# Mixture-of-experts layer on one core: the tests for optional rows turned round

## The chip, the cores and the metric

One core of one Trainium2 chip runs the whole kernel in one launch. The core has a matmul engine (TensorE; PE in the profile, its weight loads PEld), a vector engine (DVE), a scalar engine (ACT), a general engine (POOL) and a sync engine (SP) that mostly issues DMAs. Each engine follows its own instruction list with a sequencer of its own; a trailing q (PEldq) marks a row of the sequencer. The metric is the device time of the launch in microseconds (us), as the median of several runs.

## The reference

An attention part and a mixture of experts over 4096 tokens of 512 numbers. Each token goes to 2 of 8 experts; an expert takes at most 1280 rows.

```python
x = x + _L0_xcond_ref(_layernorm(x), ctx_2048, ctx_2048, itok_B_779_1933)
x = x + _L0_ffn_ref(_layernorm(x), L0_ffn_Wg, L0_ffn_w1, L0_ffn_w2)

# _L0_ffn_ref, E = 8 experts, K = 2, C = 1280 rows at most
probs = jax.nn.softmax(xr @ Wg, axis=-1)
gate_vals, expert_idx = jax.lax.top_k(probs, K)
dispatched = xr[dispatch_mask.reshape(-1) % S].reshape(E, C, d)
h = jax.nn.relu(jnp.einsum('ecd,edf->ecf', dispatched, w1))   # 512 -> 2048
expert_out = jnp.einsum('ecf,efd->ecd', h, w2)                # 2048 -> 512
out = jnp.einsum('ks,ksm->sm', combine_weights, rerouted)
```

How many rows an expert really gets is known only while the kernel runs.

## The kernel before

The first part (to about 705 us of the span) is attention, routing and the writing of each token's row to a buffer ordered by expert. The second part, `experts`, is what the change touches. It handles the experts one after the other. An expert's rows come as two full tiles of T = 512 rows, numbered n = 2e and 2e + 1, and an optional rest of up to 256 rows, cut into ENDS = 4 end blocks of HP = 64 rows.

A full tile is done in NF = 16 steps. `up(n, f)` multiplies the rows with a piece of w1: 12 matmuls (four chunks, each as three products of high and low parts, lines 1408 to 1410), into the PSUM bank `ps_h`. ScalarE takes the relu (`relu`, line 1147, tile `hhi`), VectorE the low part (`low`, line 1269, tile `hlo`). `down(n, f)` multiplies these with a piece of w2: 12 matmuls (lines 1427 to 1429) into `ps_y`. On TensorE `up` of a step is written ahead of `down` of the step before, so that the other two engines work beside it.

After the first tile's steps (t = 0) the next tile's first `up(n + 1, 0)` is issued, and then comes the optional part. Here `rows`, a register that each of TensorE, VectorE and ScalarE loads for itself, is tested. The paths are:

- no rest (`rows <= 2 * T`): the tile's last `down(n, 15)`, then `end_skipped(e, 0)`, which counts three semaphores up (line 994) as the blocks would have;
- one block (up to 64 rows): `down(n, 15)`, `end_block(e, 0)` and `end_skipped(e, 1)`. On TensorE a block is 32 matmuls on w1 (line 1442), 16 transposes (line 1453) and 32 matmuls on w2 (line 1464). Its `end_skipped` waits until the counters show all of the block's work as done (`skipped`, the wait ahead of each increment), the last one `ed_done`, the end of line 1464's matmuls;
- four blocks: `down(n, 15)` and four times `end_block`.

Whichever path is taken, TensorE goes on with `up(n + 1, 1)` at its end. VectorE scales the finished tile (`y_out`, line 1311) and the end rows (`y_out_end`, lines 1319 to 1329); POOL adds them to the output with indirect DMAs.

The order on an engine is the order of the code: there is no scheduler. All three paths of an expert stand in the instruction list one behind the other, and branches choose among them. A branch to a path or to the code behind the paths is taken by the engine's sequencer; the engine itself works meanwhile on what the sequencer has already handed over. `down`'s first matmul in a block's `ps_y` waits on `y_ready` and `ey_ready` (the wait of line 1425 and the one above it).

Of the kernel before, what the change touches and what calls it, by code (L numbers as in the profile page):

```python
# [24 lines left out]
T = 512  # L25
TB = T // P
NF = FF // P
# [13 lines left out]
HP = P // 2  # L41
# [843 lines left out]
def experts(nc, w1, w2, out_rows, disp, totals, fill, spare, raw, raw_ld, xin, xin_ld):  # L885
    N = 2 * E
    with ExitStack() as stack:
# [238 lines left out]
        @block.scalar  # L1126
        def _(act):
            def cut(e, i):
                k = PIECES * e + i
                act.wait_ge(raw_ld[k % NRAW], 16 * (k // NRAW + 1))  # L1130
                nc.scalar.activation(piece(w1hi, w2hi, i), raw_view(raw, k), ACT.Copy).then_inc(w_hi, 1)

            def x_high(n, c):
                if n == 0:
                    act.wait_ge(x0_done, c + 1)
                else:
                    act.wait_ge(xt_done, NC4 * (n - 1) + c + 1)
                nc.scalar.activation(xhi[n % 2][:, c, :], (ps_y[c] if n == 0 else ps_x)[:], ACT.Copy).then_inc(xhi_ready, 1)

            def end_high(e, half):  # L1140
                act.wait_ge(ex_done[half], e + 1)
                nc.scalar.activation(ex[:, :, :, 0, :], ex_rows, ACT.Copy).then_inc(ehi_ready[half], 1)

            def relu(n, f):
                k = NF * n + f
                act.wait_ge(h_done, k + 1)
                nc.scalar.activation(hhi[k % 2][:], ps_h[k % 3][:], ACT.Relu).then_inc(hhi_ready, 1)  # L1147

            def end_moved(e, j, q):
                m = NC4 * (ENDS * e + j) + q  # L1150
                act.wait_ge(eu_done, m + 1)
                if j or q >= 2:
                    act.wait_ge(et_done, m - 1)
                nc.scalar.activation(hrow[q % 2], end_bank(2 * e, q)[HP:P, :], ACT.Copy).then_inc(eu_moved, 1)

            def end_cols(e, j, q):
                m = NC4 * (ENDS * e + j) + q
                act.wait_ge(et_done, m + 1)
                if j or q >= 2:
                    act.wait_ge(ed_done, m - 1)  # L1160
                nc.scalar.activation(eh[q % 2][:, :, 0, :], eh_rows, ACT.Relu).then_inc(ehh_ready, 1)

            def end_block(e, j):
                if j == 2:
                    end_high(e, 1)
                end_moved(e, j, 0)
                end_moved(e, j, 1)
                end_cols(e, j, 0)
                end_moved(e, j, 2)
                end_cols(e, j, 1)  # L1170
                end_moved(e, j, 3)
                end_cols(e, j, 2)
                end_cols(e, j, 3)

            def end_skipped(e, j):
                if j <= 2:
                    skipped(act, ehi_ready[1], e, 1)
                skipped(act, eu_moved, NC4 * (ENDS * e + j), NC4 * (ENDS - j))
                skipped(act, ehh_ready, NC4 * (ENDS * e + j), NC4 * (ENDS - j))

            for i in range(2):
                cut(0, i)
            for c in range(NC4):
                x_high(0, c)
            for e in range(E):
                rows = rows_of(act, e)
                for t in range(2):
                    n = 2 * e + t
                    for f in range(NF):
                        if not (t == 1 and f == 0):  # L1190
                            relu(n, f)
                        if n == 0 and f % 2 == 0 and f < NF - 2:
                            cut(0, f + 2)
                            cut(0, f + 3)
                        if f in XAT and n + 1 < N:
                            x_high(n + 1, XAT.index(f))
                        if t == 0 and f == ENDAT:
                            end_high(e, 0)
                        if t == 0 and e >= 1 and f == 1:
                            cut(e, PIECES - 2)  # L1200
                            cut(e, PIECES - 1)
                        if t == 1 and e + 1 < E and f % 2 and f >= 3:
                            cut(e + 1, f - 3)
                            cut(e + 1, f - 2)
                    if t == 0:
                        relu(n + 1, 0)
                        with act.If(rows > 2 * T):
                            with act.If(rows > 2 * T + HP):
                                for j in range(ENDS):
                                    end_block(e, j)  # L1210
                            with act.Else():
                                end_block(e, 0)
                                end_skipped(e, 1)
                        with act.Else():
                            end_skipped(e, 0)

        @block.vector
        def _(dve):
# [118 lines left out]
            for e in range(E):  # L1337
                rows = rows_of(dve, e)
                for t in range(2):
                    n = 2 * e + t  # L1340
                    for f in range(NF):
                        if not (t == 1 and f == 0):
                            low(n, f)
                        if t == 0 and f == 0 and e >= 1:
                            y_out(n - 1)
                        if n == 0 and f % 2 == 0 and f < NF - 2:
                            cut(0, f + 2)
                            cut(0, f + 3)
                        if f + 1 in XAT and n + 1 < N:
                            x_turn(n + 1, XAT.index(f + 1))  # L1350
                        if f in XAT and n + 1 < N:
                            x_low(n + 1, XAT.index(f))
                        if t == 0 and f == ENDAT - 1:
                            end_turn(e, 0)
                        if f == 3 and n + 1 < N:
                            keep_gates(n + 1)
                        if t == 0 and f == ENDAT:
                            end_low(e, 0)
                            keep_end_gates(e)
                        if t == 0 and e >= 1 and f == 1:  # L1360
                            cut(e, PIECES - 2)
                            cut(e, PIECES - 1)
                        if t == 1 and e + 1 < E and f % 2 and f >= 3:
                            cut(e + 1, f - 3)
                            cut(e + 1, f - 2)
                    if t == 0:
                        low(n + 1, 0)
                        with dve.If(rows > 2 * T):
                            y_out(n)
                            with dve.If(rows > 2 * T + HP):  # L1370
                                for j in range(ENDS):
                                    end_block(e, j)
                                    y_out_end(e, j)
                            with dve.Else():
                                end_block(e, 0)
                                y_out_end(e, 0)
                                end_skipped(e, 1)
                        with dve.Else():
                            end_skipped(e, 0)
                            y_out(n)  # L1380
            y_out(N - 1)

        @block.tensor
        def _(pe):
# [98 lines left out]
            def end_skipped(e, j):  # L1483
                skipped(pe, eu_done, NC4 * (ENDS * e + j), NC4 * (ENDS - j))
                skipped(pe, et_done, NC4 * (ENDS * e + j), NC4 * (ENDS - j))
                skipped(pe, ed_done, NC4 * (ENDS * e + j), NC4 * (ENDS - j))
# [3 lines left out]
            for e in range(E):  # L1490
                rows = rows_of(pe, e)
                for t in range(2):
                    n = 2 * e + t
# [6 lines left out]
                            down(n - 1, NF - 1)  # L1500
                    if t == 0:
                        up(n + 1, 0)
                        with pe.If(rows > 2 * T):
                            with pe.If(rows > 2 * T + HP):
                                down(n, NF - 1)
                                for j in range(ENDS):
                                    end_block(e, j)
                            with pe.Else():
                                down(n, NF - 1)
                                end_block(e, 0)  # L1510
                                end_skipped(e, 1)
                        with pe.Else():
                            down(n, NF - 1)
                            end_skipped(e, 0)
            for b in range(TB):
                down(N - 1, NF - 2, [b])
                down(N - 1, NF - 1, [b])
# [21 lines left out]
```

## Time and profile before

| what | value |
|---|---|
| median of 3 runs | 2215.71 us (2215.48 to 2218.86) |
| the profiled execution's own time | 2217.91 us |
| its span, first to last instruction | 2216.2 us |
| TensorE busy (matmuls) | 2128.2 us, 96% |
| VectorE, ScalarE, POOL busy | 45%, 33%, 21% |
| mean granted TensorE clock | 0.988 of full |

The span is what the trace covers; 1.7 us of the execution's own time lie around it. TensorE's share is that of matmul records, which overlap a little. The share of the whole hides that the two parts differ: in the first, engines wait for each other, in the second TensorE stands almost without a pause.

### The profile page before, as it was taken

What the parts mean: (1) busy time and instruction counts of PE and PEld (TensorE: products, weight loads), DVE (VectorE), ACT (ScalarE), POOL (GpSimd) and SP (SyncE); (2) the same over time, 40 slices, a digit from 0 to 9 for tenths busy, and PEclk for the clock granted to TensorE, in tenths of its full rate; (3) what the DMA queues carried; (4) which work ended last, traced back from release to release, by engine and by line L of the source; (5) the groups of instructions that cost most, each with busy time, mean ns of one, the idle gap of its engine ahead of it and who ended that gap; (6) DMA issues with size and microseconds to landing.
All of it is one profiled execution on the core that took longest, in us unless ns stands there. A gap on an engine that the chain in (4) does not pass through costs nothing. (4 is left out here: it accounts for less than half of the span.)

```text
span 2216.2 us, 27023 instructions
## 1 busy us (share of the span) xinstructions
PE 2128.2 (96%) x10226; PEld 1524.4 (69%) x10226; DVE 1000.8 (45%) x1872; ACT 727.2 (33%) x1246; POOL 471.2 (21%) x595
## 2 busy tenths in 40 slices
PE   3899999999995999999999999999999999999997
PEld 1445555455544888877888888888888788888776
DVE  5577787777754434323423423432432342343211
ACT  1566666666662323212212211321321221132110
POOL 3133434434323110310201021031030102101101
PEclk9999999999996999999999999999999999999999
DMA  8987877788833444321612523432251252341101
GB/s 132 148 164 161 176 168 155 178 165 180 156 110 128 127 97 124 70 40 59 149 25 58 125 49 58 123 67 38 90 122 21 59 125 48 58 124 29 16 6 19
DMA packets 180724, 218.60 MB, mean 99 GB/s; under 512 B 35472, under 2 KB 107160, under 8 KB 180537
## 3 DMA queue, kind: packets, MB, share of 16 engines
q1 hardware_dynamic: 150852, 174.85, 36.6%
q0 software_dynamic: 22240, 37.92, 8.9%
q10 hardware_dynamic: 7476, 3.75, 1.0%
q8 instruction: 99, 1.62, 0.3%
q14 instruction: 57, 0.46, 0.1%
HBM read 113.93 MB, written 68.29 MB: 82 GB/s over the span
## 5 line engine op out<-in xcount | busy, mean ns | idle before, releaser
L1269 DVE SCALAR_TENSOR_TENSOR hlo<-ps_h,hhi 128x512 fp32r<-128x512 f32 x256 | 177.1, 692 | 931.2 <-ACT hhi L1147 879.1
L1147 ACT ACTIVATE hhi<-ps_h 128x512 fp32r<-128x512 f32 x256 | 152.9, 597 | 1123.5 <-PE ps_h L1410 1084.4
L1427 PE MATMUL ps_y<-w2hi,hhi 128*128 128x512 f32 x1024 | 404.8, 395 | 3.2 <-issue 2.5
L1408 PE MATMUL ps_h<-xhi,w1hi 128*128 128x512 f32 x1024 | 404.5, 395 | 1.3 <-PEq L994 1.3
L1429 PE MATMUL ps_y<-w2hi,hlo 128*128 128x512 f32 x1024 | 404.3, 395 | 0.0
L1428 PE MATMUL ps_y<-w2lo,hhi 128*128 128x512 f32 x1024 | 403.8, 394 | 0.0
L581 DVE TENSOR_REDUCE nmax<-ps_s 128x1 f32<-128x512 f32 x512 | 338.0, 683 | 145.3 <-PE ps_s L784 137.5
L1410 PE MATMUL ps_h<-xhi,w1lo 128*128 128x512 f32 x1024 | 403.6, 394 | 0.0
L1409 PE MATMUL ps_h<-xlo,w1hi 128*128 128x512 f32 x1024 | 403.3, 394 | 0.0
L435 ACT ACTIVATE probs<-ps_t 128x512 f32<-128x512 f32 x512 | 280.3, 600 | 197.2 <-PE ps_t L794 138.1
L1428 PEld LDWEIGHTS ps_y<-w2lo,hhi 128*128 128x128 f32 x1024 | 193.1, 189 | 48.5 <-issue 2.7
L1408 PEld LDWEIGHTS ps_h<-xhi,w1hi 128*128 128x128 f32 x1024 | 192.3, 188 | 47.9 <-issue 2.6
L784 PE MATMUL ps_s<-kst,qst 96*128 96x512 f32 x416 | 190.7, 469 | 35.7 <-DMA qst<-qlo 29.6
L1427 PEld LDWEIGHTS ps_y<-w2hi,hhi 128*128 128x128 f32 x1024 | 192.7, 188 | 46.6 <-DVE hlo L1269 1.1
L1429 PEld LDWEIGHTS ps_y<-w2hi,hlo 128*128 128x128 f32 x1024 | 192.6, 188 | 46.1
L1409 PEld LDWEIGHTS ps_h<-xlo,w1hi 128*128 128x128 f32 x1024 | 192.7, 188 | 45.5
L1410 PEld LDWEIGHTS ps_h<-xhi,w1lo 128*128 128x128 f32 x1024 | 192.3, 188 | 46.0
L1082 POOL DMA_INDIRECT out_x<-y,ids x64 | 103.4, 1616 | 455.4 <-DVE y L1311 441.0
L784 PEld LDWEIGHTS ps_s<-kst,qst 96*128 96x128 f32 x416 | 82.0, 198 | 145.6 <-DVE nmax L581 67.3
L794 PE MATMUL ps_t<-qst,kst 104*128 104x512 f32 x416 | 169.2, 412 | 3.7 <-ACT probs L435 1.6
L1064 POOL TENSOR_TENSOR ids<-xtail,zeros 128x4 int32<-128x4 int32 x15 | 5.5, 365 | 713.3 <-DMA xtail<-dispatched 713.3
L767 PE MATMUL ps_o<-probs,vt 128*32 128x512 f32 x1024 | 137.2, 608 | 0.0
(160 smaller groups left out, 2018.0 us busy)
## 6 DMA issues: line engine op xcount, KB each, us to landing
raw<-in_L_ffn_w SPq DMA_DIRECT2D x128, 512.0 KB
qst<-qhi SPq DMA_DIRECT2D x64, 256.0 KB
xin<-dispatched SPq DMA_DIRECT2D x60, 256.0 KB, 5.9
kst<-khi SPq DMA_DIRECT2D x52, 256.0 KB
xt<-in_x SPq DMA_DIRECT2D x32, 256.0 KB, 3.7
ct<-in_ctx SPq DMA_DIRECT2D x32, 256.0 KB, 3.3
qst<-qlo SPq DMA_DIRECT2D x32, 256.0 KB
xres<-in_x SPq DMA_DIRECT2D x32, 256.0 KB, 3.5
```

Of the source, the lines that this page charges most:

```text
L435: nc.scalar.activation(probs[n % 3][:, i, :], ps_t[(k - 1) % 3][:], ACT.Exp).then_inc(t_free, 1)
L581: nc.vector.tensor_reduce(nmax[s % 2][:, i, c:c + 1], ps_s[(k - 1) % 3][:], AX, ALU.max, negate=True).then_inc(s_free, 1)
L784: nc.tensor.matmul(bank[:], qst[s % KR][0:STACK, c, cols], kst[s % KR][0:STACK, c, :], start=True, stop=True).then_inc(s_done, 1)
L794: nc.tensor.matmul(bank[:], kst[g % KR][0:STACK + MROWS, i, cols], qst[g % KR][0:STACK + MROWS, i, :], start=True, stop=True).then_inc(t_d ...
L1147: nc.scalar.activation(hhi[k % 2][:], ps_h[k % 3][:], ACT.Relu).then_inc(hhi_ready, 1)
L1269: nc.vector.scalar_tensor_tensor(hlo[k % 2][:], ps_h[k % 3][:], 0.0, hhi[k % 2][:].bitcast(F32), ALU.max, ALU.subtract).then_inc(h_ready, 1)
L1408: nc.tensor.matmul(to, w1hi[:, c, fs], xhi[n % 2][:, c, :], start=(c == 0), stop=False)
L1409: nc.tensor.matmul(to, w1hi[:, c, fs], xlo[n % 2][:, c, :], start=False, stop=False)
L1410: done = nc.tensor.matmul(to, w1lo[:, c, fs], xhi[n % 2][:, c, :], start=False, stop=(c == NC4 - 1))
L1427: nc.tensor.matmul(ps_y[b][:], hhi[k % 2][:, bs], w2hi[:, f, :], start=(f == 0), stop=False)
L1428: nc.tensor.matmul(ps_y[b][:], hhi[k % 2][:, bs], w2lo[:, f, :], start=False, stop=False)
L1429: done = nc.tensor.matmul(ps_y[b][:], hlo[k % 2][:, bs], w2hi[:, f, :], start=False, stop=(f == NF - 1))
```

## The change

The tests are written the other way round on ScalarE, VectorE and TensorE, and their bodies change places. Each path contains the same operations in the same order; which rows take which path is unchanged. What changes is where each path stands in the instruction list and which path is reached or left by a jump.

```diff
@@ block.scalar
                         relu(n + 1, 0)
-                        with act.If(rows > 2 * T):
-                            with act.If(rows > 2 * T + HP):
+                        with act.If(rows <= 2 * T):
+                            end_skipped(e, 0)
+                        with act.Else():
+                            with act.If(rows <= 2 * T + HP):
+                                end_block(e, 0)
+                                end_skipped(e, 1)
+                            with act.Else():
                                 for j in range(ENDS):
                                     end_block(e, j)
-                            with act.Else():
-                                end_block(e, 0)
-                                end_skipped(e, 1)
-                        with act.Else():
-                            end_skipped(e, 0)
@@ block.vector
                         low(n + 1, 0)
-                        with dve.If(rows > 2 * T):
+                        with dve.If(rows <= 2 * T):
+                            end_skipped(e, 0)
                             y_out(n)
-                            with dve.If(rows > 2 * T + HP):
+                        with dve.Else():
+                            y_out(n)
+                            with dve.If(rows <= 2 * T + HP):
+                                end_block(e, 0)
+                                y_out_end(e, 0)
+                                end_skipped(e, 1)
+                            with dve.Else():
                                 for j in range(ENDS):
                                     end_block(e, j)
                                     y_out_end(e, j)
-                            with dve.Else():
-                                end_block(e, 0)
-                                y_out_end(e, 0)
-                                end_skipped(e, 1)
-                        with dve.Else():
-                            end_skipped(e, 0)
-                            y_out(n)
@@ block.tensor
                         up(n + 1, 0)
-                        with pe.If(rows > 2 * T):
-                            with pe.If(rows > 2 * T + HP):
+                        with pe.If(rows <= 2 * T):
+                            down(n, NF - 1)
+                            end_skipped(e, 0)
+                        with pe.Else():
+                            with pe.If(rows <= 2 * T + HP):
+                                down(n, NF - 1)
+                                end_block(e, 0)
+                                end_skipped(e, 1)
+                            with pe.Else():
                                 down(n, NF - 1)
                                 for j in range(ENDS):
                                     end_block(e, j)
-                            with pe.Else():
-                                down(n, NF - 1)
-                                end_block(e, 0)
-                                end_skipped(e, 1)
-                        with pe.Else():
-                            down(n, NF - 1)
-                            end_skipped(e, 0)
```

Per expert TensorE's list holds the four-block path (332 matmuls), the one-block path (92) and the path without a rest (12). A matmul is two instructions there, a weight load and the multiplication. With the waits and increments between them the four-block path is 686 instructions long, the one-block path about 190, the shortest about 28.

First place: TensorE, at the first expert's tests, behind `up(1, 0)`. Before:

```order
L1410 MATMUL ps_h<-xhi,w1lo 128x512
L1503 COMPARE_AND_BRANCH
L1504 COMPARE_AND_BRANCH
L1427 MATMUL ps_y<-w2hi,hhi 128x512
L1428 MATMUL ps_y<-w2lo,hhi 128x512
```

Now:

```order
L1410 MATMUL ps_h<-xhi,w1lo 128x512
L1503 COMPARE_AND_BRANCH
L1427 MATMUL ps_y<-w2hi,hhi 128x512
L1428 MATMUL ps_y<-w2lo,hhi 128x512
L1429 MATMUL ps_y<-w2hi,hlo 128x512
```

Before, the matmuls that follow the tests belong to the four-block path; now they belong to the path without a rest, and the second test stands behind that path.

Second place: TensorE, where the one-block path ends (line 1464 is its last product). Before:

```order
L1464 MATMUL ps_y<-w2hi,xhi 128x512
L1464 MATMUL ps_y<-w2lo,xhi 128x512
L1508 UNCONDITIONAL_BRANCH
L1427 MATMUL ps_y<-w2hi,hhi 128x512
L1428 MATMUL ps_y<-w2lo,hhi 128x512
```

Now:

```order
L1464 MATMUL ps_y<-w2hi,xhi 128x512
L1464 MATMUL ps_y<-w2lo,xhi 128x512
L1507 UNCONDITIONAL_BRANCH
L1427 MATMUL ps_y<-w2hi,hhi 128x512
L1428 MATMUL ps_y<-w2lo,hhi 128x512
```

The rows read alike, but what the branch passes over differs. Before, behind it stands the path without a rest (12 matmuls); now the four-block path (332 matmuls).

Third place: TensorE, where the path without a rest ends. Before:

```order
L1427 MATMUL ps_y<-w2hi,hhi 128x512
L1428 MATMUL ps_y<-w2lo,hhi 128x512
L1429 MATMUL ps_y<-w2hi,hlo 128x512
L1512 UNCONDITIONAL_BRANCH
L1408 MATMUL ps_h<-xhi,w1hi 128x512
```

Now:

```order
L1427 MATMUL ps_y<-w2hi,hhi 128x512
L1428 MATMUL ps_y<-w2lo,hhi 128x512
L1429 MATMUL ps_y<-w2hi,hlo 128x512
L1503 UNCONDITIONAL_BRANCH
L1507 COMPARE_AND_BRANCH
```

Before, this path stood last and its branch led to the next instruction, `up(n + 1, 1)` (line 1408). Now it stands first and its branch leads past both other paths.

## Rows read from the trace of the kernel before

**Rows 1.** The page, part 1: busy us (share of the span), instructions

```profile
PE 2128.2 (96%) x10226; PEld 1524.4 (69%) x10226; DVE 1000.8 (45%) x1872; ACT 727.2 (33%) x1246; POOL 471.2 (21%) x595
```

**Rows 2.** Waits of the matmul engine from 716 us to the end

```profile
PE ps_y L1427 <- issue: 2.5, 1, 2.5
PE ps_h L1408 <- PEq L994: 1.3, 3, 0.4
PE ps_y L1427 <- DVE hlo L1269: 0.7, 1, 0.7
```

**Rows 3.** Windows: length, then busy us (count) of each engine, PEclk

```profile
core 0: us, PE busy (x) PEld busy (x) DVE busy (x) ACT busy (x) POOL busy (x), PEclk, DMA share, GB/s
1184.00:1355.00 171.00, 171.00 (x736) 137.67 (x735) 58.26 (x74) 38.08 (x56) 27.19 (x23) 1.00 0.37 81
800.99:805.15 4.16, 4.16 (x20) 3.37 (x18) 0.11 (x1) 0.00 (x0) 0.00 (x0) 1.00 0.03 8
1354.96:1359.13 4.17, 4.17 (x19) 3.35 (x18) 0.10 (x1) 0.00 (x0) 0.00 (x0) 1.00 0.02 4
2093.94:2098.27 4.33, 4.33 (x13) 3.37 (x13) 2.07 (x3) 0.00 (x0) 1.45 (x1) 0.61 0.01 4
```

**Rows 4.** Groups by line: one end block's first product

```profile
L1442 PE MATMUL ps_h<-w1hi,ex 128*128 128x512 f32 x48 | 19.6, 408 | 0.0
```

**Rows 5.** Source L1503, TensorE's sequencer: ns min/median/max, first and last start

```profile
L1503 PEldq COMPARE_BRANCH  x8: 82/3316/3632, 801.0 to 2087.2; - x8
```

**Rows 6.** Source L1504, the second test's branch

```profile
L1504 PEldq COMPARE_BRANCH  x3: 3338/3373/3573, 979.3 to 2087.3; - x3
```

**Rows 7.** Source L1508, the branch at an end block's end

```profile
L1508 PEldq COMPARE_BRANCH  x3: 185/185/190, 1003.6 to 2115.8; - x3
```

**Rows 8.** Source L1503 from 800 to 802 us

```profile
L1503 PEldq COMPARE_BRANCH  x1: 3307/3307/3307, 801.0 to 801.0; - x1
```

**Rows 9.** DMA from 800.99 to 804.30 us, during that branch

```profile
q8 instruction: 1, 0.02, 1.7%
```

**Rows 10.** DMA from 1003 to 1005 us, around an L1508 branch

```profile
DMA packets 0, 0.00 MB, mean 0 GB/s; under 512 B 0, under 2 KB 0, under 8 KB 0
```

**Rows 11.** Source L1207: ScalarE's first branch

```profile
L1207 ACTq COMPARE_BRANCH  x8: 40/45/53, 805.4 to 2091.5; - x8
```

**Rows 12.** Timeline around 2091 us: start, length, instruction [idle before]

```profile
2091.09 0.40 PE L1410 MATMUL ps_h<-xhi,w1lo 128*128 128x512 f32 x1
2091.09 0.19 PEld L1427 LDWEIGHTS ps_y<-w2hi,hhi 128*128 128x128 f32 x1
...
2093.94 0.39 PE L1427 MATMUL ps_y<-w2hi,hhi 128*128 128x512 f32 x1 [2.46 <-issue]
```

**Rows 13.** DMA from 2090.68 to 2094.20 us

```profile
q8 instruction: 1, 0.02, 2.4%
```

**Rows 14.** DMA from 1184 to 1355 us, 736 matmuls and 735 loads

```profile
q8 instruction: 6, 0.10, 0.2%
```

**Rows 15.** Timeline around 1003 us, the end of an end block

```profile
1003.04 0.40 PE L1464 MATMUL ps_y<-w2lo,xhi 128*128 128x512 f32 x1
...
1003.88 0.50 PE L1408 MATMUL ps_h<-xhi,w1hi 128*128 128x512 f32 x1 [0.44 <-PEq L994]
...
1004.99 0.48 DVE L1329 TENSOR_SCALAR y_end<-y_part,end_gates 64x512 f32<-64x512 f32 x1
```

**Rows 16.** Source L994 from 1179.3 to 1180 us

```profile
L994 PEldq EVENT_SEMAPHORE  x3: 51/51/51, 1179.4 to 1179.7; - x3
```

**Rows 17.** Timeline at 97 us, TensorE

```profile
97.07 0.50 PE L784 MATMUL ps_s<-kst,qst 96*128 96x512 f32 x1 [4.41 <-DVE nmax L581]
```

**Rows 18.** Windows: 97.5 to 104.3 us, PEclk the third from the right

```profile
97.50:104.30 6.80, 6.64 (x24) 2.27 (x22) 2.98 (x5) 2.39 (x5) 1.64 (x3) 0.50 0.99 153
```

## The prediction

> **What bounds the kernel now.** I read the page's first part: TensorE is busy 96% of the span, no other engine half of it [rows 1]. That is an average over two parts, so I went to TensorE's waits from 716 us on, the part that the change touches [rows 2]. The reader is to see three rows with 4.5 us in all: one wait of 2.5 us ended by "issue" (no engine was late, the instruction itself was), three of 0.4 us behind an end block, and one of 0.7 us at the end. So a microsecond that TensorE loses there is a microsecond of the result, and nothing else in it matters unless it makes TensorE wait. A window inside the part gives the step: 736 matmuls in 171.0 us, 0.232 us each, at the full granted clock [rows 3].
>
> Next: which path do the experts take? Line 1442's first product ran 48 times [rows 4] and a block has 16 of them: three blocks. The first test ran eight times [rows 5], the second three times [rows 6]. So three experts (tests at 979, 1713 and 2087 us) have one block, five have none, and none has four.
>
> Then the branches of TensorE's sequencer. Three of the first tests (the minimum of 82 ns) were not taken; the five that jumped over the blocks took up to 3632 ns [rows 5], and the three second tests, which jump over the four-block path, took 3338, 3373 and 3573 ns [rows 6]. The branch behind a block, which passes only the path without a rest, took 185 to 190 ns [rows 7]. The first long one (3307 ns, [rows 8]) has one packet of an instruction queue, 0.02 MB, inside it [rows 9]; around a short one there is no DMA at all [rows 10]. I read this as: a jump far ahead leaves the instructions that the sequencer holds and waits until a block of them has been read from memory, 3.3 to 3.6 us. The branch of line 1512 has no record: it led to the next instruction. ScalarE's branches took 40 to 53 ns [rows 11]; its paths are short, VectorE's too, and they were jumped over before as well, so I put both engines at nothing. If one of them had a far jump, its 3.3 us would show in TensorE's wait for `ey_ready`.
>
> The Trainium skill ("Runtime: NRT & Kernel Launch", Instruction fetch mechanics) says that a taken branch to a target outside the current two pages forces a DMA of the target page before execution goes on. The trace agrees (3307 ns and one packet against 185 ns and none). The same section gives TensorE room for 2048 instructions, by which a jump over 686 could land in what is there; that reading is rival B.
>
> **What hid these 3.3 us.** The sequencer runs ahead of the engine. When the first long branch began, TensorE had 4.16 us of work before it, and when the fourth expert's began 4.17 us (18 matmuls at 0.232; [rows 3]). 3.31 to 3.63 us fit below that, and TensorE did not stop. It stopped once, in the last expert's second test: the branch ended at 2087.30 + 3.37 = 2090.67, one weight load passed at 2091.09, and the matmul that belongs to it started at 2093.94 [rows 12], with a second instruction packet in between [rows 13]. A packet holds some 250 instructions (six packets in a stretch of 736 matmuls and 735 loads, [rows 14]); the jump's target lay one or two instructions ahead of the end of such a packet, so the sequencer had to wait for the next one, until 2093.94 − 2090.67 = 3.27 us after the branch.
>
> **The change, part by part.**
>
> (a) The stall of the last expert goes. Its second test now falls through, and the first jumps only over the 28 instructions of the short path, as the 0.19 us branches did. Gained: 2093.94 − 2091.09 = 2.85, less one step of 0.23: 2.62 us. Behind the stall the granted clock was at its lower level (1.2 instead of 2.4 GHz, mean 0.61 over the window): 12 steps took 4.33 us instead of 12 × 0.232 = 2.79 [rows 3]. That is 1.54 us more. Sum −4.16.
>
> (b) The three one-block experts now leave the block by a jump over 686 instructions. Nothing covers it: `end_skipped` waits for `ed_done`, that is until line 1464's last matmul has finished, so the queue is empty when the branch comes. In the first block: last matmul started at 1003.04, next matmul 1003.88 [rows 15], the branch of 0.19 us right ahead of it. The price is a long branch instead of a short one. I take the three of line 1504, which jump over the same code: 3.34 + 3.37 + 3.57 − 3 × 0.19 = +9.7 us. Bounds: 3 × (3.31 − 0.19) = 9.4 and 3 × (3.63 − 0.19) = 10.3. Behind the branch wait `up(n + 1, 1)`, and with it ScalarE and VectorE; no engine has other work for TensorE. VectorE's end rows, done at 1004.99 + 0.48 = 1005.47 [rows 15], are ready before TensorE resumes at about 1007.1, so their wait costs nothing.
>
> (c) The clock after (b). TensorE now idles 0.6 + 3.2 = 3.8 us at each of three places. After 2.6 us of idleness it fell once, for 1.54 us of loss; after 4.4 us at 97 us [rows 17] it stayed at the lower level for 6.8 us [rows 18], which at this step would cost twice as much, 3.1; after the 0.6 us pauses it did not fall. So the price of each place lies between 0 and 3.1. I take the nearest row, 1.54, in two of three places, since that fall does not tell me where the limit is: +3.1 in all.
>
> (d) The five experts without a rest. Before, the far branch stood ahead of `down(n, 15)`; now behind it and behind three increments, which come 0.15 us apart, 0.35 us together [rows 16]. `down` replaces `up` as cover: 4.16 − 0.35 = 3.8 us against branches of 3.31 to 3.63. Price 0, at most 0.1 each if the longest branch meets the shortest cover. If the cover were gone, each would cost what (b) does, 3.2.
>
> (e) A second packet after a jump. All eight far jumps now land at `up(n + 1, 1)`. Placing the packets' ends by the stall at 2091 us and counting instructions, I get at least 39 instructions to the end of the packet at every landing, the least in the last expert. 39 instructions are 19 matmuls or 4.5 us, more than the 3.27 us that the second packet takes. Price 0; if the count is off, up to 4.2 us at one landing.
>
> Sum: −4.2 + 9.7 + 3.1 + 0 + 0 = +8.6 us. Against the profiled execution's own 2217.9 us that is 2226.5. That execution lies 2.2 us above the median of the runs shown, so I put the sum on the median: 2215.7 + 8.6 = 2224.3 us. The lower end of the costs (no clock fall, 9.4) gives +5.2, so 2220.9; the upper end with every place at 1.54 and 10.3 gives +10.7, so 2226.4, and 2229 if the stall of (a) is not in the unprofiled runs. That mechanism's own range is thus 2220.5 to 2229.5.
>
> **Rivals.**
>
> A. Exposed further: the far branch of the five short paths is not covered after all, or a landing is short of instructions. For: the margin of (d) is 0.2 us where a branch takes 3.6. Against: the cover was the same 4.16 to 4.17 us in two experts and the sequencer's lead does not depend on which matmuls fill it. Price: one landing 4.2, or pauses of 0.1 to 1 us with a lower clock after some; 2224.3 + 5 = about 2229. Chance 0.12.
>
> B. Not slower: the jump behind the block is as cheap as it was. This would be so if TensorE's sequencer kept the code that it has passed over, or if a branch without a test had its target read ahead. It is decided at one place, the branch behind line 1464: if it takes 0.19 us, (b) and (c) vanish and (a) stays, 2215.7 − 4.2 = 2211.5, just within 0.2%. Against it: all eight jumps over 686 instructions or more took 3.3 us and more. For it: no unconditional branch of this length is in the trace. Chance 0.08.
>
> C. Half of it: the branch overlaps with the drain (its target is asked for while `ed_done` is still awaited), or the clock never falls and the branches are at their shortest, so that less than 4.4 us is left. 2215.7 + 3 = 2218.7. Nothing in the trace speaks for the overlap; the short branch began after the last increment. Chance 0.08.
>
> **How the numbers follow.** The forecast holds 0.72, A 0.12, B 0.08, C 0.08. 0.2% (4.4 us) is about what a measurement of this kernel can tell from no change. Forecast and A are slower by more, 0.84, with a third of C 0.86; faster by more needs B and a little luck, 0.02; the rest, 0.12, is within. The range that leaves out 2 in 10 is 2219 to 2230: it takes in both ends of (b) and (c), and A.
>
> **What will show it.** The changed profile should have three records of line 1507's unconditional branch of 3.3 to 3.6 us, each with an instruction packet inside, and TensorE's wait ahead of line 1408 at 3.6 us three times instead of 0.4. The five of line 1503's short path should be as long without any pause of TensorE. The wait of 2.5 us at line 1427 should be gone and the first test's record in one-block experts about 0.19 us. PEclk should be below 1 for some 3.4 us behind two or three of the pauses. It would be wrong if line 1507's branch took 0.2 us, or if pauses appeared behind line 1503.

## The result and the profile after

The changed kernel takes 2229.09 us (median of 6 runs, 2224.41 to 2231.65) against 2216.18 us before (6 runs, 2215.07 to 2218.92). The ratio is 1.0052, 95% interval 1.0037 to 1.0067: slower by 8 to 15 us. The forecast was 2224.3 us in a range of 2219 to 2230, with 0.86 on slower. The profiled execution took 2231.13 us, its span 2229.4 us, 13.2 us over the span before.

TensorE's waits of the changed kernel from 716 us on:

```profile
PE ps_h L1408 <- issue: 11.2, 3, 3.9
PE ps_y L1427 <- DVE hlo L1269: 0.7, 1, 0.7
```

Of [rows 2] the single wait of 2.5 us at line 1427 is gone, and the three of 0.4 us at line 1408 have become three of 3.5 to 3.9. These are the branches of line 1507 behind the three end blocks; the sequencer's rows, each from a stretch of its own (ns, then first and last start):

```profile
L1507 PEldq COMPARE_BRANCH  x1: 3265/3265/3265, 1003.1 to 1003.1; - x1
L1507 PEldq COMPARE_BRANCH  x1: 3516/3516/3516, 1741.9 to 1741.9; - x1
L1507 PEldq COMPARE_BRANCH  x1: 3643/3643/3643, 2122.6 to 2122.6; - x1
```

[Rows 7] had 185 to 190 ns for the branch at that place. Inside the first of them, 1003.1 to 1006.3 us, one instruction packet was read, and a second in the 2.6 us behind it (the two DMA views):

```profile
q8 instruction: 1, 0.02, 1.9%
```

```profile
q8 instruction: 1, 0.02, 3.0%
```

The timeline around the first, beside [rows 15]:

```profile
1002.50 0.40 PE L1464 MATMUL ps_y<-w2lo,xhi 128*128 128x512 f32 x1
1003.00 0.69 DVE L1319 COPY y_part<-ps_y 64x512 f32<-64x512 f32 x1 [3.15 <-PEq L994]
...
1004.44 0.48 DVE L1329 TENSOR_SCALAR y_end<-y_part,end_gates 64x512 f32<-64x512 f32 x1
...
1006.41 0.79 PE L1408 MATMUL ps_h<-xhi,w1hi 128*128 128x512 f32 x1 [3.51 <-issue]
1007.00 0.63 PE L1409 MATMUL ps_h<-xlo,w1hi 128*128 128x512 f32 x1
...
1007.43 0.63 PE L1410 MATMUL ps_h<-xhi,w1lo 128*128 128x512 f32 x1
```

VectorE is through at 1004.92; nothing but the sequencer holds TensorE back until 1006.41. Then the matmuls come 0.43 us apart instead of 0.23. The windows behind the three pauses, up to the first step at full speed (length, busy us and count by engine, PEclk third from the right):

```profile
1006.41:1012.44 6.03, 6.03 (x15) 4.74 (x15) 0.00 (x0) 0.51 (x1) 2.33 (x2) 0.51 0.13 17
1745.46:1749.69 4.23, 4.23 (x12) 3.31 (x13) 0.00 (x0) 0.00 (x0) 1.53 (x1) 0.60 0.16 22
2126.34:2131.98 5.64, 5.64 (x14) 4.44 (x14) 0.00 (x0) 0.11 (x1) 1.73 (x2) 0.51 0.16 22
```

The granted clock was at its lower level (1.2 instead of 2.4 GHz) behind all three. The five experts without a rest show no pause. The first one's far branch took 3397 ns and ended at 802.85 + 3.40 = 806.25, and `up(n + 1, 1)` followed `down(n, 15)` at the usual step:

```profile
L1503 PEldq COMPARE_BRANCH  x1: 3397/3397/3397, 802.8 to 802.8; - x1
```

```profile
806.29 0.39 PE L1429 MATMUL ps_y<-w2hi,hlo 128*128 128x512 f32 x1
806.52 0.40 PE L1408 MATMUL ps_h<-xhi,w1hi 128*128 128x512 f32 x1
```

In the three experts with a block line 1503's branch now passes only the short path; in the first of them it took 263 ns, and the stall of [rows 12] is nowhere:

```profile
L1503 PEldq COMPARE_BRANCH  x1: 263/263/263, 978.5 to 978.5; - x1
```

### The profile page after: what moved, and what is told of

The parts are those of the page before. It is cut to its first block and busy times, and to the rows that moved or that the text cites. A ratio compares the mean times of both kernels' runs of the same rounds, so it can differ in the third digit from the quotient of the medians.

```text
span 2229.4 us, 27038 instructions
## 1 busy us (share of the span) xinstructions
PE 2134.1 (96%) x10226; PEld 1526.3 (68%) x10226; DVE 998.6 (45%) x1872; ACT 727.2 (33%) x1246; POOL 471.7 (21%) x595
```

## The experiments

Each ratio is to the kernel before, measured on the same chip beside the variant: median 2216.93 us for the first four, 2219.11 us for the others. The spread between single runs of one kernel is up to 14 us, so where one place is in question its rows are read, not the times.

**Which engine: TensorE alone.**

```diff
 # block.tensor as in the changed kernel; block.scalar and block.vector as before
-                        with pe.If(rows > 2 * T):
+                        with pe.If(rows <= 2 * T):
```

> Only TensorE's tests are turned round, ScalarE's and VectorE's stay as before. My theory (the loss is TensorE's uncovered far jump behind an end block, and the granted clock after it): as in the changed kernel, +9 to +14 us over before, three pauses of 3.9 to 4.3 us ahead of line 1408. Rival (the other engines' new jumps delay what TensorE waits for): under +4 us.

Measured: 2227.65 us, ratio 1.0053 (1.0040 to 1.0067), the same as with all three engines (1.0052). Waits of TensorE:

```profile
PE ps_h L1408 <- issue: 12.0, 3, 4.1
PE ps_y L1427 <- DVE hlo L1269: 0.7, 1, 0.7
```

**The other two engines alone.**

```diff
 # block.scalar and block.vector as in the changed kernel; block.tensor as before
-                        with act.If(rows > 2 * T):
+                        with act.If(rows <= 2 * T):
```

> Only ScalarE's and VectorE's tests are turned round, TensorE's stay as before. My theory: no difference from before, within 1.5 us, and TensorE's stall of 2.6 us in the last expert is still there. Rival (those engines carry part of the loss): +3 us or more.

Measured: 2216.37 us, ratio 1.0005 (0.9996 to 1.0015), no difference. The stall of the last expert is there:

```profile
PE ps_y L1427 <- issue: 3.0, 1, 3.0
PE ps_h L1408 <- PEq L994: 1.3, 3, 0.4
```

Together the two say that the loss is in TensorE's list; what the other two engines add is at most the 3 us that the second interval leaves (1.0015).

**Distance: the code that is jumped over made short.** In this kernel TensorE's four-block path does one block; no expert takes it here.

```diff
                             with pe.Else():
                                 down(n, NF - 1)
-                                for j in range(ENDS):
-                                    end_block(e, j)
+                                end_block(e, 0)
+                                end_skipped(e, 1)
```

> The changed kernel, with TensorE's four-block path (that no expert takes here) cut to one block, so 192 instructions instead of 686; for an expert that needs four blocks it would leave three out. The jump behind an end block passes 192 instructions instead of 686. My theory (price by distance: outside what the sequencer holds): the three branches of line 1507 fall from 3.3 to 3.6 us to 0.2, the clock falls there vanish, and with the last expert's old stall gone too the time is 3 to 5 us under before. Rival 1 (an unconditional or second branch costs 3.3 us whatever it passes): still +9 us or more. Rival 2 (the pause is the drain of ed_done that the profile puts on the branch): pauses as long as in the changed kernel.

Measured: 2213.81 us, ratio 0.9988 (0.9976 to 1.0001), 14 us under the changed kernel by the two ratios (1.0052 − 0.9988, of 2216). Against before that is −2.7 us (−5.3 to +0.2), a little less than the 3 to 5 expected and hardly told from no change. The profiled run has no pause as in the changed kernel, and no fall of the clock: its steps of over 0.3 us lose 3.4 us less than those of the kernel before. The branches behind the blocks took 308 to 313 ns, not the 0.2 us expected, and TensorE's waits there are up to 0.7 us; this is the first branch, and the waits:

```profile
L1507 PEldq COMPARE_BRANCH  x1: 312/312/312, 999.6 to 999.6; - x1
```

```profile
PE ps_h L1408 <- PEq L994: 1.8, 3, 0.7
```

So the 3.3 us are not in a branch without a test, nor in the drain, but in how far ahead the branch leads. The same run has a finer answer in the five experts without a rest, where the jump now leads 385 instructions ahead, more than one packet and less than two:

```profile
L1503 PEldq COMPARE_BRANCH  x1: 3489/3489/3489, 799.4 to 799.4; - x1
```

```profile
L1503 PEldq COMPARE_BRANCH  x1: 3793/3793/3793, 1174.6 to 1174.6; - x1
```

```profile
L1503 PEldq COMPARE_BRANCH  x1: 309/309/309, 1353.8 to 1353.8; - x1
```

```profile
L1503 PEldq COMPARE_BRANCH  x1: 765/765/765, 1532.7 to 1532.7; - x1
```

```profile
L1503 PEldq COMPARE_BRANCH  x1: 308/308/308, 1908.8 to 1908.8; - x1
```

One and the same jump took 0.3, 0.8 or 3.5 to 3.8 us. I count instructions in the built list from the packet's end that the stall at 2091 us gives, with 256 to a packet (the number is worked out below, at the kernel with 24 increments). By that count the two dear ones land in the next packet but one and the three others in the next. The one of 765 ns started nine instructions behind a packet's end; that the next packet was still on its way is my reading and was not tested. What counts is how many packets a jump goes ahead, not its length. The same count sorts every jump of TensorE behind 716 us in all ten profiles: within its packet 185 to 267 ns, into the next 292 to 313 ns (and the 765), further 3265 to 3892 ns. It also says why the branches behind the blocks took 0.3 us here and 0.19 before: they now cross one packet's end.

**Alignment: everything 32 instructions later.**

```diff
                     for f in range(NF):
+                        if n == 0 and f == 8:
+                            for _ in range(PAD):        # PAD = 32
+                                pe.sem_inc(pad, 1)
                         if not (t == 1 and f == 0):
                             up(n, f)
```

> The kernel before with 32 semaphore increments more on TensorE's list in the first expert, so that everything behind them lies 32 instructions later. My theory (the stall at the last expert's jump comes from a target one or two instructions ahead of the end of a fetched packet): the target now lies some 226 instructions ahead of an end, the 2.6 us stall and the 3.4 us of lower clock vanish, 3 to 5 us under before; the 32 increments take 1.6 us of the sequencer and are hidden by its lead of 4.1 us. Rival (the stall is a wait for another engine or a slow read of instructions in that place): it stays, no difference or +1 us.

Measured: 2211.20 us, ratio 0.9979 (0.9968 to 0.9989), 4.7 us (2.4 to 7.1) under before. The 32 increments were not quite hidden; TensorE waited 0.7 us for them:

```profile
PE ps_h L1410 <- PEq L996: 1.3, 3, 0.4
PE ps_y L1429 <- DVE hlo L1271: 0.7, 1, 0.7
PE ps_h L1410 <- issue: 0.7, 1, 0.7
```

(Lines are two further down in this kernel.) The stall at line 1427, now 1429, is gone.

**Alignment: 24 instructions, to bring the stall back elsewhere.**

```diff
-PAD = 32
+PAD = 24
```

> As the kernel with 32 increments, but 24. By my count of instructions the last expert's target then lies 234 instructions ahead of a packet's end, and the target in the sixth expert (at about 1717 us) two. My theory: no stall at 2091, and one of 2.6 to 3.2 us ahead of line 1427's first matmul behind the sixth expert's test instead. Rival (32 increments helped for another reason): no stall anywhere, or still at 2091.

There is one execution of it (2222.49 us), the profiled one; a single time says nothing here, the place is what counts. The sixth expert's test, timeline of TensorE:

```profile
1718.78 0.39 PE L1412 MATMUL ps_h<-xhi,w1lo 128*128 128x512 f32 x1
1721.96 0.39 PE L1429 MATMUL ps_y<-w2hi,hhi 128*128 128x512 f32 x1 [2.79 <-issue]
```

It is the only long wait of that run's second part. The stall moved from the eighth expert to the sixth, as counted. It also gives the packet's length. An expert takes 2444 instructions of the list before, so from the one place to the other it is 2 × 2444 − 24 = 4864 instructions. Both targets lie just ahead of a packet's end, so this is a whole number of packets, and near the 250 of [rows 14] only 19 × 256 fits.

**Cover: work beside the far jump of the changed kernel.**

```diff
-                        if not (t == 1 and f == 0):
+                        if not (t == 1 and f < 2):
                             up(n, f)
...
                                 end_block(e, 0)
+                                up(n + 1, 1)
                                 end_skipped(e, 1)
```

and the same line ahead of `end_skipped(e, 0)` and behind the four blocks.

> The changed kernel with up(n + 1, 1), 12 matmuls or 2.8 us, moved from behind the paths to the end of each path, ahead of end_skipped, so that TensorE has work while the far jump is taken. My theory: the pauses behind the three end blocks shrink by about 2.8 us, from 3.3 to 3.7 of idleness beyond the old 0.6 to about 1 us each, with fewer falls of the clock; in the sixth expert the jump by my count lands 7 instructions ahead of a packet's end, so there a second wait of about 2.5 us comes on top. Time 3 to 9 us under the changed kernel. Rival (the time goes to the branch whatever runs beside it): as the changed kernel.

Measured: 2219.74 us, ratio 1.0002 (0.9993 to 1.0011). By the two ratios that is 0.5%, 11 us (7 to 15), under the changed kernel, at the upper end of the 3 to 9 expected or above it. In the profiled pair the steps of over 0.3 us lose 9.9 us less. Waits:

```profile
PE ps_y L1427 <- issue: 2.9, 3, 1.2
PE ps_y L1429 <- issue: 2.6, 1, 2.6
```

The branches are as long as ever (3297, 3672 and 3292 ns), but three waits of up to 1.2 us are left of 3.5 to 3.9. The second row is the short landing in the sixth expert; only there did the clock fall:

```profile
1736.99 0.47 PE L1427 MATMUL ps_y<-w2hi,hhi 128*128 128x512 f32 x1 [1.23 <-issue]
1737.30 0.39 PE L1428 MATMUL ps_y<-w2lo,hhi 128*128 128x512 f32 x1
1740.28 0.59 PE L1429 MATMUL ps_y<-w2hi,hlo 128*128 128x512 f32 x1 [2.59 <-issue]
```

**The same cover in the kernel before.** The edit is the same, in the old order of the paths.

```diff
                                 end_block(e, 0)
+                                up(n + 1, 1)
                                 end_skipped(e, 1)
```

> The kernel before with up(n + 1, 1) moved likewise into the paths. It covers the drain behind an end block: the three pauses of 0.6 us go (1.8 us in all). The move makes each expert's part of TensorE's list longer; by my count the stall of 2.6 us or more then stands in the second expert (at about 980 us) and no longer in the last. Time 1 to 3 us under before. Rival: the stall stays at 2091 us.

Measured: 2216.65 us, ratio 0.9989 (0.9979 to 0.9999), 2.4 us (0.2 to 4.7) under before. The pauses behind the blocks are gone and the stall stands in the second expert:

```profile
978.93 0.40 PE L1410 MATMUL ps_h<-xhi,w1lo 128*128 128x512 f32 x1
981.50 0.39 PE L1427 MATMUL ps_y<-w2hi,hhi 128*128 128x512 f32 x1 [2.17 <-DVE hlo L1269]
```

The profile names VectorE's `hlo` here, as the last semaphore of this wait:

```profile
980.00 0.69 DVE L1269 SCALAR_TENSOR_TENSOR hlo<-ps_h,hhi 128x512 fp32r<-128x512 f32 x1 [4.88 <-ACT hhi L1147]
```

That `hlo` belongs to `up(n + 1, 0)`, which this matmul does not read, and it was done at 980.69, 0.8 us before the matmul started. By this and by the count the wait is the sequencer's here too. A smaller wait, 0.6 us, is left in the sixth expert, whose jump lands 18 instructions ahead of a packet's end. It was not forecast.

**Cover and alignment together.** The calls of `up(n + 1, 1)` stand at the ends of the paths as in the kernel above.

```diff
+                        if n == 0 and 1 <= f <= 8:
+                            for _ in range(PAD):        # PAD = 3
+                                pe.sem_inc(pad, 1)
-                        if not (t == 1 and f == 0):
+                        if not (t == 1 and f < 2):
                             up(n, f)
```

> The same with 24 increments more, three ahead of each of eight steps of the first tile, chosen by count so that no far jump that is taken lands fewer than 86 instructions ahead of a packet's end. No stall, no pause behind the end blocks, no fall of the clock in the second part: 5 to 8 us under before, the best of all. If the alignment is not what matters: 2 us under before.

Measured: 2212.03 us, ratio 0.9961 (0.9947 to 0.9975), 8.6 us (5.5 to 12) under before, where 5 to 8 were expected, and the best of all. The clock did not fall between 716 and 2190 us. TensorE's only wait from 716 us on is the one at the end:

```profile
PE ps_y L1429 <- DVE hlo L1271: 0.7, 1, 0.7
```

## Why the prediction was right, point by point

**Bound.** TensorE's lost time is the result's: the steps of over 0.3 us in its second part add 12.4 us more beyond the ordinary step than before, and the span grew by 13.2 (the last section has the rest).

**(a) The stall goes, −4.2.** It did, with its clock fall. Its cause, a jump's target one or two instructions ahead of a packet's end, was an inference when it was written. The two alignment runs show it: 32 instructions of shift remove it, 24 move it two experts earlier.

**(b) The uncovered far jump, +9.7.** Measured from start to start: last matmul of the block to the first of line 1408, 3.91, 4.16 and 4.29 us in the three experts (1002.50 to 1006.41 in the first), against 0.84, 0.83 and 0.83 before: 12.36 − 2.50 = +9.9. The other two:

```profile
1741.30 0.40 PE L1464 MATMUL ps_y<-w2lo,xhi 128*128 128x512 f32 x1
1745.46 0.50 PE L1408 MATMUL ps_h<-xhi,w1hi 128*128 128x512 f32 x1 [3.77 <-issue]
```

```profile
2122.05 0.40 PE L1464 MATMUL ps_y<-w2lo,xhi 128*128 128x512 f32 x1
2126.34 0.80 PE L1408 MATMUL ps_h<-xhi,w1hi 128*128 128x512 f32 x1 [3.89 <-issue]
```

Mechanism and size as forecast. That it is the distance (the short four-block path), that it is TensorE's alone (the two runs by engine), and that it hurts because nothing runs beside it (the cover) are each shown by a run.

**(c) The clock behind it, +3.1.** This is the term that was mis-sized. I took the fall behind the 2.6 us stall as the price and two falls of three. All three pauses brought one, and two were longer: 14 steps in 6.03 us, 11 in 4.23 and 13 in 5.64, where 0.233 each is 3.26, 2.56 and 3.03. Less 0.1 each, by which the first step behind a block's pause was longer before too, that is 2.7 + 1.6 + 2.5 = 6.8 us. The bound of 3.1 a place that [rows 17, 18] gave would have held all three; the middle was too low. The upper end of the range did not use that bound either: it took 1.54 a place, +10.7 in all, or 2226.4 us. With 3.1 a place it would have been −4.2 + 10.3 + 9.3 = +15.4. That 2229.1 still lies inside 2219 to 2230 is owed to room that was put there for other things, the stall of (a) missing outside the profiled run and rival A, neither of which came about. In that the range was lucky.

**(d) The five short paths, 0.** Right: no pause. The margin in the first was 806.52 − 806.25 = 0.27 us. In the covered version of the changed kernel, one such branch took 3.7 us and cost 0.3 us.

**(e) The second packet, 0.** Right for all eight landings. The counting behind it held in every run where it was asked: the sixth expert in two kernels, the second in one. The limit of 39 was on the safe side: in the kernel before, landings 22 and 26 instructions ahead of a packet's end (first and sixth expert) brought no wait, while 18 brought 0.6 us, seven 2.6 and two 2.2 to 3.0.

**Sum.** −4.2 + 9.9 + 6.8 = +12.5, with 12.4 in the trace. The median moved by 12.9, the forecast was +8.6; of the 4.3 us between, 3.7 are term (c) and 0.2 term (b).

**Rivals.** B (the jump is as cheap as the short one) fell at its own deciding point: 3265 to 3643 ns, not 190. The Trainium skill's rule ("Runtime: NRT & Kernel Launch", Instruction fetch mechanics) of a window of two pages fits all branches seen here. The 2048 instructions that the section gives TensorE don't fit, since a jump 385 instructions ahead took 3.5 us; the measurement decides. C (overlap with the drain) fell with the same rows: the branch began 0.6 us behind the start of the last matmul (1003.1 against 1002.50) and took its whole length; its other form, a clock that never falls, did not occur either. A (pauses in the short paths) did not occur in the changed kernel. Might the stall of (a) be in the profiled run only? The kernel with the shift, 4.7 us faster by the ratio over all runs, speaks for its being in the others too.

## What to carry to other kernels

On TensorE here a jump beyond the next instruction packet took 3.3 to 3.9 us of sequencer time. Whether that costs the kernel anything depends on what the engine still has in its queue when the jump comes. So put such a jump where work is queued, not behind a wait that has just drained the engine; "the common case first" is not the rule. Where such jumps exist, count where they land: here a shift of 32 instructions was worth 4.7 us, and any edit to the engine's list moves the landings.

## What the hardware showed unexpectedly

- How long the clock stays low is not set by the pause alone. After waits of 2.5 us (before) and 3.8 us (the second pause of the changed kernel) TensorE was back at its full step 3.9 and 4.2 us later; after waits of 3.5 and 3.9 us only 6.0 and 5.6 us later. In the kernel with TensorE's tests alone turned round, two waits of 4.05 us were followed by 3.1 and by 5.6 us. After the 2.2 us in the second expert of the old order with cover it had never left it. What decides between them stays open.
- The ordinary step of TensorE has two values. From 1190 to 1345 us, without a pause in it, the kernel with 32 increments did 670 matmuls and the kernel before 667 (windows of the two kernels):

```profile
1190.00:1345.00 155.00, 155.00 (x670) 125.72 (x669) 54.38 (x68) 36.27 (x53) 22.88 (x20) 1.00 0.38 86
```

```profile
1190.00:1345.00 155.00, 155.00 (x667) 124.80 (x666) 54.40 (x68) 36.29 (x53) 22.10 (x20) 1.00 0.38 86
```

  Within a run the step keeps its value over hundreds of matmuls; counted over 256 of them it is 59.37 or 59.66 us. Over the second part's 6384 matmuls that is up to 7 us, which may be much of the spread between runs. In the profiled pair the mean ordinary step made the changed kernel 2 us longer, and the first part, 1.4 us shorter in that run, gave most of that back. It was not tested what sets it.
